# Two attention layers on one core: the selection scores multiplied from unstacked rows, with three edits to the order beside them

## The reference

```python
# layer 0, for each image: n = 1024 tokens, 8 heads of 16
x_norm = layernorm(x) * ln_scale + ln_bias
q, k, v = split(x_norm @ w_qkv + b_qkv)
attn = softmax(einsum('bqhd,bkhd->bhqk', q, k) * 16 ** -0.5)
x = x + einsum('bhqk,bkhd->bqhd', attn, v).reshape(b, n, c) @ w_out + b_out
# layer 1
tokens = x @ Win + b_in
t = layernorm(tokens) * g1 + be1
q, k, v = heads(t @ Wq), heads(t @ Wk), heads(t @ Wv)
pk, pv = pool2d(k), pool2d(v)                       # 4x4 means: 64 positions
scores = einsum('bhsd,bhpd->bhsp', q, pk)           # the selection scores
red = scores.max(axis=(1, 2))                       # over heads and tokens
_, top_idx = top_k(red, 16)
attn = softmax(einsum('bhsd,bhkd->bhsk', q, pk[top_idx]) * scaling)
tokens = tokens + einsum('bhsk,bhkd->bhsd', attn, pv[top_idx])
tokens = tokens + gelu(layernorm(tokens) @ Wf1 + bf1) @ Wf2 + bf2
out = tokens @ Wout + bout
```

## Time and profile before

| | us |
|---|---|
| median of 3 runs | 860.02 |
| lowest and highest | 855.59, 860.54 |
| the profiled execution | 855.3 |
| its span in the profile | 853.6 |
| TensorE busy | 796.4 (93%) |
| ACT busy | 603.8 (71%) |
| DVE busy | 519.4 (61%) |
| POOL busy | 163.7 (19%) |
| mean granted TensorE clock | 0.972 |

### The profile page before, as it was taken

The page is one execution under the profiler, slowest core; times in us unless marked ns, Lnnn a source line. Parts: engine busy times, 40 slices in busy tenths (PEclk is TensorE's granted clock), DMA queues, the critical chain, the costliest instruction groups (busy, mean ns, idle before and its releaser), DMA issues.

```text
span 853.6 us, 14509 instructions
## 1 busy us (share of the span) xinstructions
PE 796.4 (93%) x5155; PEld 382.9 (45%) x5155; DVE 519.4 (61%) x1518; ACT 603.8 (71%) x683; POOL 163.7 (19%) x198
## 2 busy tenths in 40 slices
PE   8889888999999999999999999999999989899988
PEld 6322332345443545345434544344533534246675
DVE  6405434678567775678567765767467853467464
ACT  3697775777887788777886788768876787682112
POOL 1620520410341031220241033202111011000100
PEclk9999987999999999999999999999999999899979
DMA  3553341422442251432342352323152232201300
GB/s 67 96 90 65 64 81 31 100 47 49 82 98 46 48 87 45 104 63 48 66 109 45 52 97 66 75 48 63 26 122 47 43 66 50 56 7 31 76 1 25
DMA packets 45309, 52.91 MB, mean 62 GB/s; under 512 B 15920, under 2 KB 33968, under 8 KB 45232
## 3 DMA queue, kind: packets, MB, share of 16 engines
q1 hardware_dynamic: 45232, 51.92, 31.3%
HBM read 5.45 MB, written 4.19 MB: 11 GB/s over the span
## 4 chain that ended last, share of the span: by engine, by line
PE 61%; ACT 13%; DVE 8%; issue 5%; ACTq 0%; DVEq 0%
PE O L631 21%; PE S L616 13%; ACT Pr L850 9%; PE BC L645 6%; PE BC L637 3%; PE S L834 3%; PE BC L742 2%; PE BC L682 2%; PE BC L728 2%; PE A L569 2%; PE BC L664 2%; DVE rsel L1159 1%; DVE rgt L1158 1%; ACT hT L890 1%; ACT L850 1%
## 5 line engine op out<-in xcount | busy, mean ns | idle before, releaser
L850 ACT ACTIVATE Pr<-S 128x1024 f32<-128x1024 f32 x512 | 491.0, 1029 | 136.3 <-PE S L616 132.8
L631 PE MATMUL O<-Pr,Va 128*32 128x512 f32 x2048 | 263.7, 623 | 8.5 <-DVE OT L1067 7.8
L616 PE MATMUL S<-Qs,Ks 49*128 49x512 f32 x1024 | 217.5, 470 | 30.2 <-ACT Pr L850 27.4
L616 PEld LDWEIGHTS S<-Qs,Ks 49*128 49x128 f32 x1024 | 87.8, 185 | 173.2 <-ACT Pr L850 132.4
L631 PEld LDWEIGHTS O<-Pr,Va 128*32 128x32 f32 x2048 | 51.9, 111 | 117.1 <-issue 96.3
L496 POOL TENSOR_TENSOR q1l<-q1T,q1h 128x1024 fp32r<-128x1024 f32 x8 | 19.1, 2389 | 226.5 <-DVE q1h L1117 226.5
L1141 DVE TENSOR_REDUCE r<-BC 128x1 f32<-128x512 f32 x64 | 41.3, 684 | 29.8 <-PE BC L682 29.4
L1067 DVE STREAM_TRANSPOSE OT<-O 128x512 f32<-128x512 f32 x32 | 22.8, 713 | 55.1 <-PE O L631 54.9
L459 POOL TENSOR_SCALAR xn<-X,ln 128x128 f32<-128x128 f32 x56 | 45.8, 830 | 3.9 <-DVE ln L980 3.9
L865 ACT ACTIVATE tT<-BC,cols 128x512 f32<-128x512 f32 x32 | 23.4, 779 | 31.5 <-PE BC L637 31.4
L510 POOL TENSOR_TENSOR tokx<-tokx_new,tok_bias 128x1024 f32<-128x1024 f32 x8 | 18.9, 2366 | 121.0 <-DVE tokx_new L986 121.0
(11 more groups left out here) (189 smaller groups left out, 995.6 us busy)
## 6 DMA issues: line engine op xcount, KB each, us to landing
Qs<-qh SPq DMA_DIRECT2D x128, 64.0 KB, 2.3
Ks<-kh SPq DMA_DIRECT2D x128, 64.0 KB, 2.3
Q1s<-q1h SPq DMA_DIRECT2D x64, 128.0 KB, 2.4
X<-in_x_dram SPq DMA_DIRECT2D x8, 512.0 KB, 4.0
Qs<-ql SPq DMA_DIRECT2D x64, 64.0 KB, 2.4
Ks<-kl SPq DMA_DIRECT2D x64, 64.0 KB, 2.3
attnT<-On SPq DMA_DIRECT2D x128, 32.0 KB, 2.0
Q1s<-q1l SPq DMA_DIRECT2D x32, 128.0 KB, 2.4
```

Of the source, the lines that this page charges most:

```text
L616: mm = pe.matmul(S[:, c, a * HALF:(a + 1) * HALF], Ks[head, j, kb * P:(kb + 1) * P], Qs[head, j, c * HALF:(c + 1) * HALF], start=True, sto ...
L631: mm = pe.matmul(O[r:r + 32, :], Va[:, kb, 2 * j + a, :], Pr[:, (STEPS * n + s) % 3, c, a * HALF:(a + 1) * HALF], start=(kb == 0), stop=(k ...
L850: act.activation(Pr[:, g % 3, c, :], S[:, c, :], ACT.Exp, scale=SCALE).then_inc(probs_ready, 1)
```

## The change

It does five things.

- **Scores without stacks.** Q1s, K1s, the tripled weight, `stack1` and the semaphore `q1_stacked` go. q1h and q1l are read where they lie, 32 rows for a pair. k1h and k1l are 128 rows by 2 heads by 64, made by DVE straight from the bank with two masked instructions each (four instructions in place of six). A step of `at.sc` takes both banks and adds three products into each: k1h q1h, k1l q1h, k1h q1l, in turns between the two banks, 24 products for an image. The pooled keys take one product where there were four.
- **One step earlier.** In `USUAL` the scores stand at steps 17 to 20, `rt` at 21, `rb` at 22, `sel` at 25 (before: 18 to 21, 22, 23, 26).
- **Squares behind the ranks.** From image 2 on `square` also waits for `hot_ready`.
- **Single sums in image 1.** Its steps below 13 add the sum of the step before, each.
- **Fewer fillers in the tail.** `WARM` at t 28 to 8, at sel 8 to 4, at pt 16 to 12, at t2 22 to 20, at out 8 to 0. The 36 at the first scores stay.

```diff
+LIGHT = 13
 After = namedtuple("After", "tok norm1 t q1 pk sc rt rb sel s2 exp2 e2 pt tok2 norm2 tt2 t2 ff gelu wout out")
-USUAL = After(tok=3, norm1=8, t=12, q1=13, pk=15, sc=(18, 19, 20, 21), rt=22, rb=23, sel=26, s2=27, exp2=28, e2=28, pt=30,
+USUAL = After(tok=3, norm1=8, t=12, q1=13, pk=15, sc=(17, 18, 19, 20), rt=21, rb=22, sel=25, s2=27, exp2=28, e2=28, pt=30,
...
-def one_by_one(n):
-
-    return n in (0, IMAGES - 1)
+def sums_behind(n, s):
+
+    if n in (0, IMAGES - 1) or (n == 1 and s < LIGHT):
+        return (s - 1,) if s > 0 else ()
+    return (s - 2, s - 1) if s % 2 == 0 and s > 0 else ()
...
-WARM = {ENDING.tok: 4, ENDING.t: 28, ENDING.pk: 8, ENDING.sc[0]: 36, ENDING.sel: 8, ENDING.pt: 16, ENDING.t2: 22, ENDING.out[0]: 8}
+WARM = {ENDING.tok: 4, ENDING.t: 8, ENDING.pk: 8, ENDING.sc[0]: 36, ENDING.sel: 4, ENDING.pt: 12, ENDING.t2: 20}
...
-            def stack1(n):
-
-                for part, q in enumerate((q1h, q1h, q1l)):
-                    if part == 0:
-                        sp.wait_ge(q1h_ready, n + 1)
-                    if part == 2:
-                        sp.wait_ge(q1l_ready, n + 1)
-                    for j in range(PAIRS):
-                        r = 2 * HD * j
-                        sp.dma_start(Q1s[2 * HD * part:2 * HD * (part + 1), j, :].bitcast(fp32), q[r:r + 2 * HD, :].bitcast(fp32))\
-                            .then_inc(q1_stacked, 16)
...
             def square(n):
 
                 wait(a_drained, a_after(n, "k", 1))
+                if n > 1:
+                    wait(hot_ready, n - 1)
...
-                    for j in range(PAIRS):
-                        mm = pe.matmul(bank[0:ROWS1, j * POS:(j + 1) * POS], wk3[:, j, :, :].rearrange("p a b -> p (a b)"),
-                                       pooled[:, :], start=True, stop=True)
-                    mm.then_inc(filled, 1)
+                    pe.matmul(bank[:, 0:POS], wkv1_s[:, 0:C], pooled[:, :], start=True, stop=True).then_inc(filled, 1)
...
-                for j in range(PAIRS):
-                    if s != at.sc[j]:
+                for u in range(PAIRS):
+                    if s != at.sc[u]:
                         continue
-                    if j == 0:
+                    if u == 0:
                         b_ready(n, K_PK)
-                        pe.wait_ge(q1_stacked, 16 * STACK1_DMAS * (n + 1))
-                    for h in range(2):
-                        bank, filled = b_turn(n, K_SC + 2 * j + h)
-                        pe.matmul(bank[:, :], K1s[:, j, :, :].rearrange("p a b -> p (a b)"), half(Q1s[0:ROWS1, j, :], h),
-                                  start=True, stop=True).then_inc(filled, 1)
+                        pe.wait_ge(q1l_ready, n + 1)
+                    banks = [b_turn(n, K_SC + 2 * u + i) for i in range(2)]
+                    for part, (k1, q1) in enumerate(((k1h, q1h), (k1l, q1h), (k1h, q1l))):
+                        for i, (bank, filled) in enumerate(banks):
+                            pair = slice(2 * HD * (u // 2 * 2 + i), 2 * HD * (u // 2 * 2 + i + 1))
+                            mm = pe.matmul(bank[:, :], k1[pair, :, :].rearrange("p a b -> p (a b)"), half(q1[pair, :], u % 2),
+                                           start=(part == 0), stop=(part == PARTS - 1))
+                            if part == PARTS - 1:
+                                mm.then_inc(filled, 1)
...
-                    if s > 0 and (s % 2 == 0 or one_by_one(n)):
-                        if not one_by_one(n):
-                            weighted(n, s - 2)
-                        weighted(n, s - 1)
+                    for behind in sums_behind(n, s):
+                        weighted(n, behind)
...
-                    keys = bank[0:ROWS1, 0:PAIRS * POS].rearrange("p (j k) -> p j k", j=PAIRS)
-
-                    def place(rows1, part):
-
-                        for a in range(2):
-                            ins = dve.tensor_scalar(K1s[rows1, :, a, :], part[rows1, :, :].bitcast(fp32),
-                                                    pair_mask[rows1, a:a + 1], None, ALU.mult)
-                        return ins
-                    low = slice(2 * HD, 4 * HD)
-                    step(own, dve.tensor_copy(k1h[:, :, :], keys))
-                    dve.tensor_tensor(k1l[low, :, :], keys[low, :, :], k1h[low, :, :].bitcast(fp32), ALU.subtract)
-                    step(own, place(slice(0, ROWS1), k1h))
-                    place(low, k1l).then_inc(drained, 1)
+                    for a in range(2):
+                        ins = dve.tensor_scalar(k1h[:, a, :], bank[:, 0:POS], pair_mask[:, a:a + 1], None, ALU.mult)
+                    step(own, ins)
+                    for a in range(2):
+                        ins = dve.scalar_tensor_tensor(out=k1l[:, a, :], in0=bank[:, 0:POS], scalar=pair_mask[:, a:a + 1],
+                                                       in1=k1h[:, a, :].bitcast(fp32), op0=ALU.mult, op1=ALU.subtract)
+                    ins.then_inc(drained, 1)
```

More of the change, by code:

```diff
@@ L383, in _ @@
                              (G1, col(g1, 0)), (BE1, col(be1, 0)), (G2, col(g2, 0)), (BE2, col(be2, 0)),
-                             (cols[:, 8:9], col(bf1, 0)), (cols[:, 9:10], col(bf1, C)),
-                             *((wk3[:, :, i, :], Wk.rearrange("c (j e) -> c j e", j=PAIRS)) for i in range(PARTS))):
+                             (cols[:, 8:9], col(bf1, 0)), (cols[:, 9:10], col(bf1, C))):
                 sp.dma_start(dst, src).then_inc(weights_in, 16)
@@ L417, in _ @@
             store(IMAGES - 2)
-            stack1(IMAGES - 1)
             store(IMAGES - 1)
@@ L444, in _ @@
                                        pattern=[[-1, POS]], channel_multiplier=1))
-            for i in range(PARTS):
-                step(8 + i, pool.tensor_copy(pair_mask[2 * HD * i:2 * HD * (i + 1), :], head_mask[0:2 * HD, 0:2]))
+            for j in range(1, PAIRS):
+                step(7 + j, pool.tensor_tensor(pair_mask[:, :], head_mask[:, 0:2] if j == 1 else pair_mask[:, :],
+                                               head_mask[:, 2 * j:2 * j + 2], ALU.add))
             step(11, pool.iota(iota_i[:, :], pattern=[[1, TOPK]], base=0, channel_multiplier=0))
@@ L493, in q1_rest @@
                 wait(q1h_ready, n + 1)
-                if n > 0:
-                    wait(q1_stacked, 16 * STACK1_DMAS * n)
                 pool.tensor_tensor(q1l[:, :], q1T[:, :], q1h[:, :].bitcast(fp32), ALU.subtract).then_inc(q1l_ready, 1)
@@ L818, in image @@
                         after_tasks(n - 1, s)
-                if not one_by_one(n):
-                    weighted(n, STEPS - 2)
-                weighted(n, STEPS - 1)
+                for behind in sums_behind(n, STEPS):
+                    weighted(n, behind)
             image(0)
@@ L1119, in after_tasks @@
                     bank, drained = drain_b(n, K_PK)
-                    keys = bank[0:ROWS1, 0:PAIRS * POS].rearrange("p (j k) -> p j k", j=PAIRS)
-                    def place(rows1, part):
-                        for a in range(2):
-                            ins = dve.tensor_scalar(K1s[rows1, :, a, :], part[rows1, :, :].bitcast(fp32),
-                                                    pair_mask[rows1, a:a + 1], None, ALU.mult)
-                        return ins
-                    low = slice(2 * HD, 4 * HD)
-                    step(own, dve.tensor_copy(k1h[:, :, :], keys))
-                    dve.tensor_tensor(k1l[low, :, :], keys[low, :, :], k1h[low, :, :].bitcast(fp32), ALU.subtract)
-                    step(own, place(slice(0, ROWS1), k1h))
-                    place(low, k1l).then_inc(drained, 1)
+                    for a in range(2):
[5 more added lines that the diff above has]
+                    ins.then_inc(drained, 1)
                     bank, drained = drain_b(n, K_PV)
                     dve.tensor_copy(pkv[:, :], bank[0:POS, 0:2 * C]).then_inc(drained, 1)
-                for j in range(PAIRS):
-                    if s != at.sc[j]:
+                for u in range(PAIRS):
+                    if s != at.sc[u]:
                         continue
-                    for h in range(2):
-                        k = K_SC + 2 * j + h
+                    for i in range(2):
+                        k = K_SC + 2 * u + i
                         bank, drained = drain_b(n, k)
-                        ins = dve.tensor_reduce(r8[:, 2 * j + h:2 * j + h + 1], bank[:, :], AX.X, ALU.max)
+                        ins = dve.tensor_reduce(r8[:, 2 * u + i:2 * u + i + 1], bank[:, :], AX.X, ALU.max)
                         if k < K_RT - 1:
                             ins.then_inc(drained, 1)
-                    if j == PAIRS - 1:
+                    if u == PAIRS - 1:
                         step(own, ins)
```

25 lines of the change are left out of this document (9 added, 16 removed).

## The result

| | before | after |
|---|---|---|
| median, us | 859.0 (4 runs) | 831.8 (4 runs, 830.28 to 833.89) |
| the profiled execution, its span | 855.3, 853.6 | 831.24, 829.5 |
| mean granted TensorE clock | 0.972 | 0.987 |
| TensorE busy | 796.4 (93%) | 778.7 (94%) |

The ratio is 0.969, with a 95% interval from 0.9652 to 0.9729. The forecast was 834, with a range from 825 to 849.

A forecast was written before the change was run, and what follows sets the result against it. TensorE sets the pace of a usual image, with clock falls, waits and the tail priced apart. Terms 4.2 - 7.0 - 3.2 - 8.5 - 4.3 - 3.0 = -21.8 from 855.3 gave 833.5, so 834; range 825 to 849.

The forecast's parts named there:

- A: Products of usual images (layer 1 of images 0 to 5): the change costs +0.7 an image, six times +4.2.
- Rival 2: Score steps: 32-row groups don't run beside each other, six products take 1.28, not 0.70; 854; chance 0.09.
- Rival 3: Score steps: products adding into the same bank wait for the one before; +2.3 in 32 steps, 907; chance 0.04.
- rival 1: Score products: weight loads stand exposed, 0.11 added to each of 12 pairs an image; 844; chance 0.06.
- B: Ranks in usual images: no longer held by POOL's squares; step 26's wait goes, -7.0, and sums at half clock, -3.2.
- rival 4: Image 1 stays partly at half clock, squares make a new wait, or the tail's clock returns late; 842; chance 0.13.
- The median's gap: Profiled execution 4.7 under the median: laid to step 26's half-clock falls in more images; 834 forecast for the median also.
- C: Image 1, steps 0 to 12: single sums keep the clock up, 33.9 for 42.4, -8.5.
- D: Image 7, before and behind the first selection scores: stacked-row wait and half clock go, -3.7, keys -0.6, together -4.3.
- E: The tail behind the last step: fewer fillers and lighter keys against slower scores, -3.0 in all.
- t: Tail, turns of the normalised tokens: 40 fewer fillers free TensorE earlier, so the turns wait for DVE, -4.0.
- Scores: Tail: products and reductions no longer overlap, 2.4 a step, three more at half clock; 11.4 for 6.3, +5.1.

The follow-up runs named there:

- e4: The kernel before with one edit, POOL's squares wait for hot_ready from image 2 on, ranks left at step 23: 843.09 us.
- e9: The changed kernel with both banks of a selection-score step reading the same 32 rows, not two different groups of rows: 853.01 us.
- e7: The changed kernel with the old steps, no wait for hot_ready, double sums in image 1 and the old fillers (unstacking alone): 864.18 us.
- e8b: The kernel before with nine products nobody reads in image 7, ahead of the wait for the stacked rows: 855.39 us.
- e1: The changed kernel with double sums again in the first steps of image 1: 841.5 us.
- e2: The changed kernel with double sums in image 1 and four pairs of filler products in its steps 1, 5, 7, 9 and 11: 836.28 us.
- e10: The changed kernel with 5 pairs of filler products ahead of the tail's first selection scores where it has 36: 825.1 us.
- e6: The changed kernel with a step's six score products reordered, three into the first bank, then three into the second: 831.64 us.
- e11: The changed kernel with banks taken one after the other in a score step, the second awaited only after the first's three products: 828.8 us.

## Why the prediction was right

The time came out 2.2 under the forecast, and every stretch within 1.7 of its term. From trace to trace the forecast was -21.8 and the spans differ by 24.1.

- **A, the products.** Three pairs at 0.233 were to take 0.70, and took 0.68. The +0.7 an image can be read against e4, which lacks the wait too but has the stacked scores: from rgt of image 1 to rgt of image 6 are 466.3 in the changed kernel and 462.6 in e4, 0.74 an image. Rival 2 (no overlap, 1.28) is what e9 builds by force, and it costs what that rival said: 0.67 a step and 853, where the rival gave 854. Rival 3 (waits within a bank) falls with the same rows. Of rival 1 only the 0.07 of e9 could be seen, and it isn't on the path of the changed kernel.
- **B, the ranks.** rgt and rsel at 0.2 to 0.3, no wait at step 26: as forecast. The squares did hold the division (1.80, L1051), which rival 4 feared, but without effect. A + B together gave -5.5 for -6.0. The image from rank to rank was to be 0.5 shorter. Over five images it is 93.3 for 94.0 on average (466.3 for 469.9), and of these 3.6 the half clock in image 5 is 1.6, so 0.4 an image is left.
- **The median's gap.** I had read the 4.7 between the profiled run and the median as half-clock falls of B in more images. Without it the forecast for the median would have been 838. e4 bears the sum out: 15.5 at the median, where the terms were 7.0 + 3.2 + 4.7 = 14.9. The traces of e7 and e8b bear out that the falls change place. That executions near the median had more of them is still inferred.
- **C, image 1.** -10.2 for -8.5. The term was mis-sized: I put the tasks behind each other on top of 1.98 a step, and noted that TensorE's slack could take up some of them, -10.5. The time came near that, but no run shows which tasks were taken up. The mechanism is shown by e1 and e2, at 5.2 for the clock.
- **D, image 7.** -4.4 for -4.3, and e8b shows that 3.05 of it was clock.
- **E, the tail.** t -4.3 for -4.0. Scores +4.7 for +5.1: 2.44 and 2.53 for the two steps at full clock (2.4 forecast) and 3.09 and 3.28 for the others (3.0), 11.34 in all. Keys only -0.3 for -0.6, since TensorE then waits for ACT. rt to sel -1.4 for -1.5. out -2.1 for -2.0 (the last two groups of products, L719 and L726, start 2.00 apart, and stood 4.13 apart before).
- **Start.** -0.5 before image 1 that I had not foreseen. It stands in the set-up, at the projection of the first tokens: 5.37 from 13.35 on before, 4.78 from 13.46 on now. From 13.3 to 16.8 the mean clock was 0.52 before and 0.66 now. The first scores wait for their transfers as long as they did, 0.75 and 0.72. I see nothing in the change that would move the clock there, and take it for luck.

What I said too little of: that 36 fillers stay "so the removed stacking brings nothing here" was right, and it was the largest thing left to take (e10).

## What to carry to other kernels

Take a change apart before crediting it. Here the part that it is named for costs 5.6, and edits of a line or two beside it, that free a waited-for engine, keep TensorE multiplying or take idle fillers out of a chain, give 32. Where a wait of one or two us stands before many products, price the clock behind it as well, and from several executions: the profiled one showed 10.2 (7.0 + 3.2) of the 15.5 that this wait cost. When transfers or waits are removed, look at what had been laid there to cover them, since it may now be the chain itself.

## What the runs showed of the hardware

- Products in two different 32-row groups overlap whatever their order in the code, and a later one of another row group can start before an earlier one (e6, and e11 across a fulfilled wait): three and three by bank take 0.89 with the change of row group, in turns 0.91, and in one row group 1.58.
- DVE is held by POOL's squares beyond the compares: L1051, a product of two SBUF tiles, took 1.79 to 1.81 in images 1 to 6 where it takes 0.42 unheld, and its page mean went from 456 to 734 ns. The Trainium skill ("SBUF — State Buffer", "Who interferes with whom") says that a DVE instruction with two SBUF inputs contends with a GpSimd instruction that reads SBUF. rsel and L1051 agree. `rgt`, which has one tile and one column as inputs, was held as well in the kernel before (1.52 for 0.25).
- The granted clock fell to 1.2 GHz behind single waits of 1.15 us (7 of 18 at step 26, in three traces) and of 1.77 (image 7, in before and e4), and in image 1 of before behind three waits of 0.3 to 0.4 with one pair of products of 0.5 between each (105.95 to 109.03). At step 26 the waits are equally long where it fell and where it didn't. Products that nobody reads kept it at 2.4 GHz in e8b, and in e2 at three of the four places where e1 has slow sums.
